# Row maxima of an attention kernel: first maxima in pairs, the second half of a maxima row deferred, head order of the last group, and part of the causal mask on VectorE

## The reference

```
attn = softmax(Q K^T / 4)            # layer 0: all keys; layer 1: keys up to the query
out  = (attn V) Wo + bo
```

## Time and profile before

| what | us |
|---|---|
| three runs | 2005.17, 1995.55, 1993.84 (median 1995.55) |
| profiled execution, its own time | 2006.2 |
| its span | 2004.5 |
| PE busy in it | 1914.6 |
| DVE busy | 1379.2 |
| ACT busy | 1088.6 |
| POOL busy | 232.4 |

### The profile page before, as it was taken

The page is one execution under the profiler, slowest core; times in us unless marked ns, Lnnn a source line. Parts: engine busy times, 40 slices in busy tenths (PEclk is TensorE's granted clock), DMA queues, the critical chain, the costliest instruction groups (busy, mean ns, idle before and its releaser), DMA issues.

```text
span 2004.5 us, 28840 instructions
## 1 busy us (share of the span) xinstructions
PE 1914.6 (96%) x10864; PEld 975.3 (49%) x10864; DVE 1379.2 (69%) x1719; ACT 1088.6 (54%) x2177; POOL 232.4 (12%) x606
## 2 busy tenths in 40 slices
PE   6999999999999999999999999999999999999998
PEld 5888887733333333333334335744543333333436
DVE  6554544425899999999996763756787777777733
ACT  4221212122787878878775774312257777677662
POOL 1000000000000000100000100000023433333330
PEclk9999999988999999999997899999999999999999
DMA  6010100043112211112212000103312212212102
GB/s 211 1 48 0 44 1 1 10 122 90 30 32 69 49 32 31 34 31 44 44 31 54 7 8 6 54 16 83 90 33 52 47 32 52 45 35 52 30 10 87
DMA packets 79211, 87.52 MB, mean 44 GB/s; under 512 B 19072, under 2 KB 52864, under 8 KB 79072
## 3 DMA queue, kind: packets, MB, share of 16 engines
q1 hardware_dynamic: 79072, 85.67, 17.2%
HBM read 55.20 MB, written 20.71 MB: 38 GB/s over the span
## 4 chain that ended last, share of the span: by engine, by line
PE 81%; ACT 7%; DVE 4%; SPq 4%; issue 2%; DMA 2%; POOL 0%; DVEq 0%; POOLq 0%; ACTq 0%; PEldq 0%
PE ps L1498 19%; PE ps L1528 11%; PE ps L1179 8%; PE ps L1180 7%; PE ps L1181 7%; PE ps L1435 7%; ACT arena L806 6%; PE ps L1524 6%; PE ps L1356 5%; PE ps L1362 4%; PE ps L1273 3%; SPq L468 2%; SPq L466 1%; DMA slots<-arena 1%; DVE arena L1043 1%
## 5 line engine op out<-in xcount | busy, mean ns | idle before, releaser
L806 ACT ACTIVATE arena<-ps 128x512 f32<-128x512 f32 (+3 forms) x1792 | 867.7, 556 | 325.5 <-PE ps L1528 171.4
L1043 DVE TENSOR_REDUCE arena<-ps 128x1 f32<-128x1024 f32 (+3 forms) x768 | 856.1, 1153 | 181.0 <-PE ps L1362 104.8
L1498 PE MATMUL ps<-arena 128*17 128x512 f32 (+3 forms) x3584 | 439.2, 562 | 1.0 <-ACT arena L806 0.6
L1362 PE MATMUL ps<-slots 48*128 48x512 f32 x1024 | 409.7, 474 | 8.8 <-DMA slots<-kparts 4.6
L1528 PE MATMUL ps<-slots 50*128 50x512 f32 x1024 | 387.9, 459 | 24.0 <-ACT arena L806 14.7
L1528 PEld LDWEIGHTS ps<-slots 50*128 50x128 f32 x1024 | 172.7, 188 | 326.7 <-ACT arena L806 269.1
L1524 PE MATMUL ps<-slots 98*128 98x512 bf16 (+3 forms) x768 | 207.7, 328 | 9.2 <-DMA slots<-arena 5.8
L1356 PE MATMUL ps<-slots 96*128 96x512 bf16 (+3 forms) x768 | 193.6, 328 | 13.8 <-DVE arena L1046 7.7
L1362 PEld LDWEIGHTS ps<-slots 48*128 48x128 f32 x1024 | 171.8, 190 | 66.7 <-DVE arena L1043 22.9
L606 POOL TENSOR_SCALAR_AFFINE_SELECT arena<-arena 128x128 f32<-128x128 f32 x512 | 145.3, 295 | 320.3 <-ACT arena L806 312.4
L667 ACT ACTIVATE xn<-ps 128x512 f32<-128x512 f32 (+1 forms) x44 | 26.3, 598 | 259.1 <-PE ps L1181 259.1
(11 more groups left out here) (127 smaller groups left out, 1855.3 us busy)
## 6 DMA issues: line engine op xcount, KB each, us to landing
slots<-qparts SPq DMA_DIRECT2D x96, 128.0 KB, 3.6
qparts<-arena SPq DMA_DIRECT2D x32, 256.0 KB
xnT<-arena SPq DMA_DIRECT2D x256, 32.0 KB
slots<-qparts SPq DMA_DIRECT2D x96, 64.0 KB, 3.3
qparts<-arena SPq DMA_DIRECT2D x48, 128.0 KB
slots<-qparts SPq DMA_DIRECT2D x32, 192.0 KB, 3.7
w_raw<-in_wgu SPq DMA_DIRECT2D x20, 256.0 KB, 3.2
acc<-in_x SPq DMA_DIRECT2D x4, 1024.0 KB, 8.0
```

Source lines behind the costliest of these rows:

```text
L806: act.activation(prob[local % P_RING][:, q0:CH], bank(local % SP_RING)[:, q0:CH], ACT.Exp, scale=SCALE).then_inc(S["p_ready"], 1)
L1043: dve.tensor_reduce(maxes[c][:, h[0] * TPC + qt:h[0] * TPC + qt + 1], src[:, 0:w], AX_X, ALU.max).then_inc(S["x_done"], 1)
L1362: last = pe.matmul(dst[:, k0:k1], q_slot[u][r:r + ROWS[0], c, h % 2, qt * P:(qt + 1) * P].bitcast(F32R), k_slot[u][r:r + ROWS[0], k0:k1].b ...
L1498: mm = pe.matmul(bank(7)[32 * h:32 * h + DH + 1, q0:CH], v_slot[n % SLOTS][:, kt, :], prob[idx % P_RING][:, q0:CH], start=(kt == 0), stop= ...
```

## The change

Four edits, and what they need:

- **First maxima in pairs.** They start in product 13 instead of 12; two items stand behind the second quarter of a product and two behind the fourth. In layer 0 their pieces are sorted by `k0`, so that the pieces of two heads alternate: first 512 columns of the one, first 512 of the other, then the second 512 of each. `lower` moves behind the second quarter's maxima, and `ROWS_AT[0]` goes from 18 to 17.
- **Second part of a rows item deferred.** DVE writes `hi` of a rows item, then runs the whole next item (reduction or norm), and only then writes `lo` (new `rows_low`) and adds to `x_done`, without the wait for `m_ready`. Because `x_done` no longer says which item is done, PE waits for `m_ready` as well where item j-2 is a rows item.
- **Last group's heads in turn.** In the last group of layer 0 the main items go in the order 0, 2, 1, 3.
- **Masks in VectorE.** In layer 1, chunk 1, PE no longer adds the mask. DVE adds it and takes the maximum in one `tensor_tensor_reduce` (scores from PSUM, a mask of up to 1024 columns in bfloat16 from SBUF, the sum written to `w_q`, which is free by then). Chunk 0 keeps the mask product on PE.

```diff
-FIRST_MAX_AT = 12
-ROWS_AT = [18, 20]
+FIRST_MAX_AT = 13
+ROWS_AT = [17, 20]
-def main_items(causal, qc):
+def main_items(causal, qc, n=0):
+    heads = (0, 2, 1, 3) if n == GROUPS - 1 and not causal else range(HG)
 def maxima_in_product(i, k, count):
-    j = 3 * (i - FIRST_MAX_AT) + k
-    return range(j, j + 1) if i >= FIRST_MAX_AT and k < 3 and j < count else range(0)
+    j = 4 * (i - FIRST_MAX_AT) + k - 1
+    return range(j, min(j + 2, count)) if i >= FIRST_MAX_AT and k % 2 else range(0)
+def masked_by_vector(causal, c):
+    return causal and c > 0
@@ maximum (VectorE), the branch of a rows item
-                    dve.tensor_scalar(negm[c][0:NX, 0, :], mt, -1.0, None, ALU.mult).then_inc(S["mhi_done"], 1)
-                    dve.wait_ge(S["mhi_done"], n * QC + c + 1)
-                    dve.scalar_tensor_tensor(negm[c][0:NX, 1, :], mt, -1.0, low_in, ALU.mult,
-                                             ALU.subtract).then_inc(S["m_ready"], 1)
-                    dve.wait_ge(S["m_ready"], n * QC + c + 1)
-                    dve.sem_inc(S["x_done"], 1)
+                    dve.tensor_scalar(hi, src[0:NX, 0:P], -1.0, None, ALU.mult).then_inc(S["mhi_done"], 1)
+                    half_done.append((src, n, c))
+                def rows_low():          # called behind every reduction and every norm
+                    if not half_done:
+                        return
+                    src, n, c = half_done.pop()
+                    dve.wait_ge(S["mhi_done"], n * QC + c + 1)
+                    dve.scalar_tensor_tensor(low, src[0:NX, 0:P], -1.0, hi if l else hi.bitcast(F32), ALU.mult,
+                                             ALU.subtract).then_inc(S["m_ready"], 1)
+                    dve.sem_inc(S["x_done"], 1)
+                def reduce_maximum(src, n, c, qt, h, j):
+                    if masked_by_vector(l == 1, c):
+                        masked = w_q[:, 2 * (j % 2):2 * (j % 2) + 2, :].rearrange("p k f -> p (k f)")
+                        dve.tensor_tensor_reduce(out=masked[:, 0:w], in0=src[:, 0:w], in1=mask_qk[:, N - w:N], scale=1.0, scalar=LOWEST,
+                                                 op0=ALU.add, op1=ALU.max, accum_out=...).then_inc(S["x_done"], 1)
+                        return
@@ first maxima of layer 0 (VectorE)
-                            if k == 0 and i:
+                            if k == 1 and i:
                                 lower(i - 1)
@@ max_piece (TensorE)
                         pe.wait_ge(S["x_done"], j if (n, c, qt) == (GROUPS - 1, 1, None) else j - 1)
+                        m, mc, mqt, _ = all_items[j - 2]
+                        if m is not None and mqt is None:
+                            pe.wait_ge(S["m_ready"], m * QC + mc + 1)
-                                         start=True, stop=k1 < w)
-                        if k1 == w:
+                                         start=True, stop=k1 < w or masked_by_vector(causal, c))
+                        if k1 == w and not masked_by_vector(causal, c):
@@ first_maxima (TensorE)
+                    todo = [piece for piece in first if piece[0] in items]
+                    if not causal:
+                        todo.sort(key=lambda piece: piece[5])
```

More of the change, by code:

```diff
@@ L34 @@
 MASKED = -1e30
+LOWEST = -3e38
 SLOTS = 3
@@ L65, in width_f @@
     return min(P, F - j * P)
-def main_items(causal, qc):
+def main_items(causal, qc, n=0):
     kts = TPC * (qc + 1) if causal else KT
-    return [(kt, h, max(0, kt - TPC * qc) * P if causal else 0) for kt in range(kts) for h in range(HG)]
+    heads = (0, 2, 1, 3) if n == GROUPS - 1 and not causal else range(HG)
+    return [(kt, h, max(0, kt - TPC * qc) * P if causal else 0) for kt in range(kts) for h in heads]
 def weight_views(t, j):
@@ L543, in _ @@
                                    pattern=[[-1, P]], channel_multiplier=1).then_inc(const_b, 1)
-            pool.affine_select(out=mask_qk[:, :], in_=mask_qk[:, :], compare_op=ALU.is_ge, fill=MASKED, base=0,
+            pool.affine_select(out=mask_qk[:, N - P:N], in_=mask_qk[:, N - P:N], compare_op=ALU.is_ge, fill=MASKED, base=0,
                                pattern=[[-1, P]], channel_multiplier=1).then_inc(const_b, 1)
@@ L801, in attend @@
                         for c in range(QC):
-                            for i, (kt, h, q0) in enumerate(items[c]):
+                            for i, (kt, h, q0) in enumerate(main_items(l == 1, c, n)):
                                 act.wait_ge(S["s_ready"], local + 1)
@@ L1286, in _ @@
                 causal = l == 1
-                items = [main_items(causal, c) for c in range(QC)]
                 group_items = per_group[l]
@@ L1328, in tail_step @@
                         pe.wait_ge(S["x_done"], items_in_all)
+                        pe.wait_ge(S["m_ready"], GROUPS * QC)
                     last = passes(dst, xo_hi[:, c % 2, k, q], xo_lo[:, c % 2, k, q], wo_hi[:, k, :], wo_lo[:, k, :], k == 0, k == KC - 1)
@@ L1336, in _ @@
                 blocks = max_blocks(l == 1)
-                items_in_all = sum(len(b) for b in blocks)
+                all_items = [item for b in blocks for item in b]
+                items_in_all = len(all_items)
                 starts = [sum(len(b) for b in blocks[:n]) for n in range(GROUPS)]
@@ L1345, in max_piece @@
                         pe.wait_ge(S["x_done"], j - 1)
+                        pe.wait_ge(S["m_ready"], (GROUPS - 3) * QC + 2)
                         broadcast([dst[:, 0:CH], dst[:, CH:2 * CH]], c, h).then_inc(S["x_ready"], 1)
@@ L1356, in max_piece @@
                         last = pe.matmul(dst[:, k0:k1], q_slot1[u][0:ROWS[1], c, h, qt * P:(qt + 1) * P], k_slot1[u][0:ROWS[1], k0:k1],
-                                         start=True, stop=k1 < w)
-                        if k1 == w:
-                            last = pe.matmul(dst[:, w - P:w], identb[:, :], mask_qk[:, :], start=False, stop=True)
+                                         start=True, stop=k1 < w or masked_by_vector(causal, c))
+                        if k1 == w and not masked_by_vector(causal, c):
+                            last = pe.matmul(dst[:, w - P:w], identb[:, :], mask_qk[:, N - P:N], start=False, stop=True)
                     else:
@@ L1443, in first_maxima @@
                 def first_maxima(items):
-                    for piece in first:
-                        if piece[0] in items:
-                            if piece[0] == 0 and piece[-2]:
-                                pe.wait_ge(S["slot_in"][0], 16 * 12)
-                                pe.wait_ge(*((S["b_evac"], TT) if l else (S["y_evac"], TT * len(ROUNDS) + 1)))
-                            max_piece(*piece)
+                    todo = [piece for piece in first if piece[0] in items]
+                    if not causal:
+                        todo.sort(key=lambda piece: piece[5])
+                    for piece in todo:
+                        if piece[0] == 0 and piece[-2]:
+                            pe.wait_ge(S["slot_in"][0], 16 * 12)
+                            pe.wait_ge(*((S["b_evac"], TT) if l else (S["y_evac"], TT * len(ROUNDS) + 1)))
+                        max_piece(*piece)
                 if l == 0:
@@ L1515, in attend @@
                         for c in range(QC):
-                            nkt = len(items[c]) // HG
-                            for i, (kt, h, q0) in enumerate(items[c]):
+                            items = main_items(causal, c, n)
+                            nkt = len(items) // HG
+                            for i, (kt, h, q0) in enumerate(items):
                                 if i == 0:
```

32 lines of the change are left out of this document (19 added, 13 removed).

## The result

The changed kernel took 2119.2 us (median of 4 runs, 2094.58 to 2125.71), the kernel before 2000.36 beside it (4 runs). The ratio is 1.060, 95% interval 1.053 to 1.067. The direction was forecast, the size was not: 2045 was predicted, and the time lies outside the range of 2000 to 2105. In all the ratios and intervals here the executions that stand over 1.5% above the fastest of their kernel are left out (one of the kernel before, of 9706.02 us, in the job of e1 to e4, one of e8 and two of e12); the medians hold them.

The account below looks back on a forecast made before the run. TensorE (PE) was taken as the bound, VectorE close behind. The terms -16 + 47 + 23 + 0 - 15 = +39 us gave 2034.5 by the runs; 10 us for the clock made the forecast 2045, range 2000 to 2105.

Parts of the forecast that it names:

- the sum: Whole kernel: the four parts add to +39 us, 2034.5 by the runs, and 10 us for the clock make 2045.
- clock: Attention: 10 us added for some 22 us of half clock behind 28 or so new pauses, 45% of such time lost.
- the clock falls often: Rival, attention: every third new pause brings 10 to 20 us of half clock, 68 us more, 2103; chance 0.16.
- pairs: Product stage of layer 0: first maxima in pairs from product 13 end the products at 479.95, a gain of 16 us.
- pair step: Product stage of layer 0: each of 11 steps takes 3.4 us, set by DVE, with PE idle some 0.7 us.
- pause, layer 0: Attention, groups 0 to 14: PE opens the second item behind each rows item 1.57 us later, 30 times, 47 us lost.
- pause, layer 1: Attention of layer 1: deferred `lo` delays PE by 0.8 us in chunk 1 and 0.7 in chunk 0, 15 times, 23 us.
- heads: Last group of layer 0: the new head order changes nothing, 0 us, with a bound of 7 us gained or lost.
- masks: Layer 1, chunk 1: 256 mask products of 0.06 us leave PE, 15 us gained, with DVE's operation no longer.
- at best 4.5 us gained: Attention of layer 0: the deferral's bound, 30 x 0.15 us saved after `lo`, if PE weren't held at item j+2.
- half-rate rival: Layer 1, chunk 1: the combined add and maximum runs at half rate, +130 us, 2175; chance 0.06.
- PE not held: Rival, attention: the deferred half doesn't hold PE, so 1961, or 1975 with a fifth of the stall left; chance 0.16.

Follow-up runs that it names:

- e1: The changed kernel with both halves of a rows item made at once again, with the wait for m_ready; 1975.46 us, ratio 0.987 to the kernel before.
- e4: The changed kernel with both halves of a rows item made at once, PE instead of DVE waiting for m_ready; 1962.78 us, ratio 0.982.
- e8: The kernel before with only the last group's heads in turn; 1991.37 us, ratio 1.000.
- e12: The kernel e4 with the deferred half only for the rows items of chunk 0 of layer 0; 2010.04 us, ratio 1.005.
- e3: The changed kernel with dummy score products in the pauses behind rows items, six in layer 0, three in layer 1; 2051.98 us, ratio 1.029.
- e11: The changed kernel with three dummy products in each pause behind a rows item, in layer 0 and layer 1; 2064.57 us, ratio 1.033.
- e5: The kernel before with only the first maxima in pairs, from product 13; 1976.36 us, ratio 0.992.
- e7: The kernel before with only the masks of layer 1, chunk 1, in VectorE; 1982.82 us, ratio 0.993.
- e2: The kernel before with only the deferred half of a rows item; 2161.39 us, ratio 1.084.

## Why the prediction was wrong

**The step that failed** is the last line of the sum: "To this I add 10 us for the clock", where "10 us stands for some 22 us" at half clock. Measured: 235 - 44 = 191 us more of it between the first and the last copy of layer 0. The price per microsecond was near: 108.7 - 30 x 1.4 = 67 us for those 191, or 0.35, where I used 0.45; why it is less was not tested. It was the count that was wrong: 26 falls, where the sum had some 22 us for them all. I read one fall behind one pause of 1.24 us and let the many pauses without a fall outweigh it.

That reading was itself wrong in two ways. The 1.24 us in the chain are the length of DVE's reduction, and not an idle of PE; PE's own timeline has half of that at the place:

```profile
1072.81 0.51 PE L1362 MATMUL ps<-slots 48*128 48x512 f32 x1 [0.61 <-DVE arena L1043]
```

And the fall behind it did not last for the 4 us of the window in rows 11 but for 41.0 us (1073.2 to 1114.2), which alone is nearly twice the 22 us that the sum allowed for all 30 new pauses. So the trace had a long fall behind an idle of 0.61 us, and the pauses around it that were to speak against the rival were idles of 0.36 to 0.66 us (1065.57 to 1084.09), not of the 1.4 that the change makes. e1 shows that the falls go with the deferral, e12 a fall in 13 of its 15 chunks with a pause, and e3 and e11 that the falls get shorter, and somewhat fewer, as the pause is filled.

**The rival "the clock falls often"** had this mechanism and nearly this price (68 us, measured 67), and I gave it 0.16. That the prices meet is in part luck: it took 150 us of half clock at 0.45, and there were 191 at 0.35. Its sum was 2103. The 16 us above it are no further cost that the trace shows: between the two profiled executions the difference is 108.4, and the rival's is 39 + 68 = 107. The sum took off 10.65 us for the profiled run of before, which its median did not keep (a fourth run, 2007.20, raised it from 1995.55 to 2000.36), and the median of after lies 5 above its own profiled run.

**The sum, term by term:**

| step | forecast | measured | from |
|---|---|---|---|
| pairs | -16 | -17 (-15 in the whole change) | e5; first copies |
| pair step | 3.4 us | 2.96 | timeline |
| pause, layer 0 | 30 x 1.57 = 47 | 30 x 1.4 = 42 | chunks 22.8 less 21.4 |
| pause, layer 1 | 15 x 1.5 = 23 | 15 x 1.4 = 21 | chunk 0: 11.9 here, 10.5 in e1 |
| heads | 0 | 0 | e8 |
| masks | -15 | -11 | e7 |
| clock | +10 | +67 | table above |

- *Pairs.* The slot and the clock were as forecast in 440 to 465. The step was too long: I let the next pair begin when both items are reduced, but its first item has the banks that come free after the first reduction, so that PE and not DVE sets the step. What the product end of 474.84 (forecast 479.95) had won was then given back at the start of attention by a fall of 20.5 us, where 6.8 stood before.
- *Pause in layer 0.* The chain `hi`, reduction, `lo`, piece is as written, 0.2 us shorter. The bound "at best 4.5 us gained" for what the edit saves was taken at 0, and e4 does not contradict it.
- *Pause in layer 1.* The total is right, the places are not: I had +0.8 us in chunk 1 and +0.7 in chunk 0, and chunk 1 takes 18.9 us with and without the deferral while chunk 0 grows by 1.4. The two idles of a group are 29.0 / 15 = 1.9 us, of which e1 has 4.0 / 15 = 0.3 at the same pieces already.
- *Masks.* The product's 0.06 us in the chain was a little too much: 0.6 us per chunk of 16 is 0.04. The combined operation takes 1022 ns on average, the four reductions of its widths before it 1019, so that the half-rate rival is out. The accumulator read is a second instruction, as the Trainium skill says (page VectorE: DVE Perf Modes, section "Two Vector instructions with no wait between them"), and the trace agrees (256 of each); it takes 0.083 us, not my 0.28: 21 us of DVE time, and e7 shows that they cost less than the mask products did.
- *PE not held.* The 60 pauses are in the trace, so this rival is out.

The Trainium skill, page TensorE: Matmul & The Clock Gate, section "A second HAM failure mode: psum-queue depth-cycling", says that frequent very short idles between groups of products can make the clock swing between its two levels. The trace agrees in layer 0, where no pause behind `lo` is over 1.4 us and the granted clock fell 26 times between the copies. It does not in layer 1, where 30 pauses of up to 1.0 us had two falls, nor does it account for the 15 falls of e3 with no idle above 0.15 us before them. Weighed as a rule that speaks against this change, it would have moved chance from my forecast to the rival.

**Open:** what sets off a fall, since e3 has 15 in layer 0 without an idle of PE above 0.15 us before them and layer 1 has hardly any behind 30 pauses; why the clock falls for 3.4 us behind one pause and for 13.7 behind another; why e2 has more of it than the whole change; and what decides the long fall in group 13, which some executions have (38.6 to 38.9 us for its first chunk) and others not (28.9), and which makes up much of the spread of all these kernels.

## What to carry to other kernels

- Work that another engine must finish before a buffer comes free does not become cheap by being put later. Here `lo` was 0.28 us, and putting it behind a reduction of 1.23 made PE, in order, wait for both. Ask of each deferred instruction which buffer it still reads, and who stands at that buffer.
- A pause on a nearly full TensorE is to be priced twice: its own length, and the clock behind it. Here a chunk of layer 0 with a pause of 1.4 us became 1.4 to 6 us longer, while in layer 1 two pauses of 1.0 us in a group cost 1.4 us together and hardly any clock. Before the change the trace had one long fall behind an idle of 0.61 us; in this case that was reason enough to take many falls as a main case and not as a tail. The length of an idle is to be read from the engine's own timeline and not from the chain of waits, and the length of a fall to its end. Filling the pause with dummy products is the quick test that tells the two prices apart.

## What the runs showed of the hardware

- Six dummy products in each pause of layer 0 and three in each of layer 1, in an otherwise unchanged schedule, made the kernel 67 us faster (2119.2 to 2051.98), with the half clock down from 282 to 98 us. Three in each did most of that (2064.57). The falls between the copies of layer 0 went from 26 to 21 to 19 in number and from 9.1 to 5.7 to 3.6 us in mean length.
- A `tensor_tensor_reduce` (add, then maximum) with scores in PSUM and a bfloat16 mask in SBUF takes 814 to 1226 ns for 640 to 1024 columns, as a plain reduction of the same widths does (811 to 1226 in the kernel before), and the accumulator read behind it 81 to 85 ns.
